# A two-layer graph network on one core: a fourth ring buffer, low halves written over the turned block, and six groups of x projected during the first chunks

## What is computed

```
A = adj + I;  deg = sum(A, axis=1);  d = rsqrt(deg)
A_hat = A * d[:, None] * d[None, :]
x1 = layernorm(x + elu((A_hat @ x) @ w))
x2 = layernorm(x1 + relu((adj @ x1) @ W.T + b))
return x2
```

## Time and profile before

| | |
|---|---|
| median of 3 runs | 890.79 us (888.59 to 893.01) |
| the profiled execution | 887.64 us, span 885.5 us |
| TensorE busy (PE) | 793.9 us, 90% |
| VectorE busy (DVE) | 745.8 us, 84% |
| ScalarE busy (ACT) | 501.5 us, 57% |
| GpSimd busy (POOL) | 172.7 us, 20% |
| read from HBM | 176.8 MB, 204 GB/s over the span |

### The profile page before, as it was taken

One profiled execution on the slowest core, in us unless ns is written; L12 is line 12 of the kernel. 1 busy time (PEld: TensorE's weight loads), 2 busy tenths in 40 slices (PEclk: granted clock), 3 DMA queues, 4 the chain that ended last, 5 costly groups with the idle time before them and its releaser, 6 DMA issues. The chain is left out here.

```text
span 885.5 us, 10755 instructions
## 1 busy us (share of the span) xinstructions
PE 793.9 (90%) x3532; PEld 652.4 (74%) x3532; DVE 745.8 (84%) x611; ACT 501.5 (57%) x1084; POOL 172.7 (20%) x181
## 2 busy tenths in 40 slices
PE   0446959799999999899999999999999989999996
PEld 0335848578878888688887788888888878888885
DVE  2368969899999998788998999898879789888863
ACT  2254546465676673377876745766744565455352
POOL 0003341213442400022210201110210312022021
PEclk9968969899999999899999999999999999999999
DMA  9998987389999649489879778888896887997911
GB/s 272 306 304 215 255 197 172 113 214 274 228 256 281 173 128 273 131 206 227 215 186 253 199 214 202 185 222 194 195 250 172 198 216 186 220 223 171 223 29 30
DMA packets 183590, 181.72 MB, mean 205 GB/s; under 512 B 6768, under 2 KB 183536, under 8 KB 183536
## 3 DMA queue, kind: packets, MB, share of 16 engines
q1 hardware_dynamic: 94704, 93.21, 41.7%
q10 hardware_dynamic: 88832, 87.83, 40.1%
HBM read 176.82 MB, written 4.19 MB: 204 GB/s over the span
## 5 line engine op out<-in xcount | busy, mean ns | idle before, releaser
L967 PE MATMUL acc<-a_hi,v_hi 128*128 128x512 f32 x1024 | 408.6, 399 | 43.4 <-DVE a_lo L638 28.9
L452 ACT ACTIVATE a_hi<-turned 128x1024 fp32r<-128x1024 f32 x256 | 263.9, 1058 | 281.5 <-PE acc L969 126.9
L969 PE MATMUL acc<-a_hi,v_lo 128*128 128x512 f32 x1024 | 402.9, 393 | 0.0
L968 PE MATMUL acc<-a_lo,v_hi 128*128 128x512 f32 x1024 | 402.8, 393 | 0.0
L638 DVE TENSOR_TENSOR a_lo<-turned,a_hi 128x1024 fp32r<-128x1024 f32 x256 | 307.9, 1240 | 32.3 <-ACT a_hi L452 24.2
L621 DVE STREAM_TRANSPOSE turned<-raw 128x2048 f32<-128x2048 f32 x120 | 275.4, 2302 | 26.8 <-DMA raw<-in_adj_dram 21.3
L967 PEld LDWEIGHTS acc<-a_hi,v_hi 128*128 128x128 f32 x1024 | 195.2, 191 | 88.5 <-issue 32.8
L969 PEld LDWEIGHTS acc<-a_hi,v_lo 128*128 128x128 f32 x1024 | 194.7, 190 | 41.4
L968 PEld LDWEIGHTS acc<-a_lo,v_hi 128*128 128x128 f32 x1024 | 195.2, 191 | 39.8
L462 ACT ACTIVATE acc<-raw 128x256 f32<-128x256 f32 x170 | 62.7, 369 | 24.5 <-DMA raw<-in_adj_dram 21.4
L645 DVE TENSOR_REDUCE deg_parts<-raw 128x6 f32<-128x1536 f32 (+3 forms) x28 | 53.5, 1911 | 18.1 <-DMA raw<-in_adj_dram 18.1
(11 more groups left out here) (70 smaller groups left out, 416.1 us busy)
## 6 DMA issues: line engine op xcount, KB each, us to landing
raw<-in_adj_dram SPq DMA_DIRECT2D x152, 512.0 KB, 8.8
raw<-in_adj_dram ACTq DMA_DIRECT2D x152, 512.0 KB, 9.8
x_row<-in_x_dram SPq DMA_DIRECT2D x64, 128.0 KB, 7.1
out_dram<-normed ACTq DMA_DIRECT2D x28, 128.0 KB, 3.3
held<-in_adj_dram ACTq DMA_DIRECT2D x4, 512.0 KB, 12.8
held<-in_adj_dram SPq DMA_DIRECT2D x4, 512.0 KB, 12.8
partial<-in_adj_dram ACTq DMA_DIRECT2D x4, 512.0 KB, 11.9
partial<-in_adj_dram SPq DMA_DIRECT2D x4, 512.0 KB, 14.2
```

The costliest lines, as they stand in the source:

```text
L452: nc.scalar.activation(a_hi[u % 2][:, part, :], turned[u % 2][:, part, :], ACT.Copy).then_inc(s_hi, 1)
L967: pe.matmul(dst, v_hi[:, k, ch], a_hi[u % 2][:, t, :], start=begin, stop=False)
L968: pe.matmul(dst, v_hi[:, k, ch], a_lo[u % 2][:, t, :], start=False, stop=False)
L969: ins = pe.matmul(dst, v_lo[:, k, ch], a_hi[u % 2][:, t, :], start=False, stop=end)
```

## The change

1. A fourth ring buffer `raw3` (home 6). The ring is (0, 1, 6, 2) up to chunk 32 and (0, 1, 6) behind it; chunk (2, 1) has no place of its own any more.
2. `turned` has three buffers and `a_lo` lies at the same addresses: lo(u) overwrites the turned block in place. turn(u) now waits for the product of u-3; lo(u) waits only for hi(u). `a_hi` keeps two buffers.
3. New shares of the row sums: VectorE 10, 10, 6, 3, 3, 4, 4, 4 blocks, GpSimd 5 from group 2 on, ScalarE 6, 6, 5, 8, 8, 7, 7, 7. GpSimd's steps work inside `normed`.
4. x @ w of group g is made at the chunk `X_USED[g]` = 2, 3, 4, 5, 6, 7, 28, 31 for g = 0 to 7: turn_x(g) ends chunk X_USED[g]-1 on TensorE, keep_xt(g) begins ScalarE's part of chunk X_USED[g], project_x(g) begins TensorE's, and a new copy keep_y(g) ends ScalarE's. It frees `proj`: the result is kept in SBUF, in `y_soon` (inside v_lo, groups 0 to 3) or one of two `y_late` (groups 4 to 7). x is loaded straight to these places, two chunks ahead, all on SP's queue; w, W and b are loaded behind chunk 0.
5. The scratch of dynamic DMAs shrinks from 4096 to 256.

```diff
@@ -52,6 +52,7 @@
     RB = GN // B32
     EPS = 1e-5
     JUNK = 2
+    TURNS = 3
...
-    HOMES = {chunk_of[0, 1]: 3, chunk_of[1, 1]: 4, chunk_of[0, 0]: 5, chunk_of[2, 1]: 5}
+    HOMES = {chunk_of[0, 1]: 3, chunk_of[1, 1]: 4, chunk_of[0, 0]: 5}
+    RING = (0, 1, 6, 2)
     buffer_of, before, filled = [], [], []
     for n in range(len(chunks)):
         if n in HOMES:
             home = HOMES[n]
         else:
-            held = [max([k for k in range(n) if buffer_of[k] == i], default=-1) for i in range(3)]
-            free = [(done_at[k] if k >= 0 else -1, i) for i, k in enumerate(held)]
-            home = min(free[:3 if n <= FIRST_B else 2])[1]
+            free = []
+            for i in RING if n <= FIRST_B else RING[:3]:
+                k = max([k for k in range(n) if buffer_of[k] == i], default=-1)
+                free.append((done_at[k] if k >= 0 else -1, i))
+            home = min(free)[1]
...
-    DVE_BLOCKS = [10, 10, 8, 6, 5, 6, 6, 5]
-    POOL_BLOCKS, POOL_FROM = 4, 2 * PANELS
+    DVE_BLOCKS = [10, 10, 6, 3, 3, 4, 4, 4]
+    POOL_BLOCKS, POOL_FROM = 5, 2 * PANELS
+    X_USED = [2, 3, 4, 5, 6, 7, 28, 31]
...
-        turned = [sb(f"turned{i}", [P, GT, GN]) for i in range(2)]
+        raw.append(sb("raw3", [P, RB, STRIPE]))
+        turned_at = -(-nc.sbuf_base // B32) * B32
+        turned = [sb(f"turned{i}", [P, GT, GN]) for i in range(TURNS)]
         a_hi = [sb(f"a_hi{i}", [P, GT, GN], F32R) for i in range(2)]
-        a_lo = [sb(f"a_lo{i}", [P, GT, GN], F32R) for i in range(2)]
+        a_lo = [nc.alloc_sbuf_tensor_at(f"a_lo{i}", [P, GT, GN], F32R, offset=turned_at + 4 * GT * GN * i) for i in range(TURNS)]
...
-        halved = sb("halved", [P, POOL_BLOCKS, STRIPE // 2])
-        quartered = sb("quartered", [P, POOL_BLOCKS, STRIPE // 4])
-        folded = sb("folded", [P, 2, POOL_BLOCKS, STRIPE // 8])
+        halved = normed[:].rearrange("p t n -> p (t n)")[:, 0:POOL_BLOCKS * (STRIPE // 2)].rearrange("p (k m) -> p k m", k=POOL_BLOCKS)
+        folded = normed[:].rearrange("p t n -> p (t n)")[:, POOL_BLOCKS * (STRIPE // 2):POOL_BLOCKS * (STRIPE // 2 + STRIPE // 4)]
+        folded = folded.rearrange("p (i k m) -> p i k m", i=2, k=POOL_BLOCKS)
+        w_kept = partial[:, 0, :, 0:C]
+        y_late = [sb(f"y_late{i}", [P, GT, C]) for i in range(2)]
+        y_soon = nc.alloc_sbuf_tensor_at("y_soon", [P, N // P, C], F32, offset=v_at + 4 * (N // P * C))
...
+        def y_of(row):
+
+            return y_soon[:, tiles(row), :] if row < FAST else y_late[row % 2][:]
...
-                if m >= 1 and m <= GROUPS:
-                    sp.wait_ge(s_xw, m)
-                elif m > GROUPS:
+                if m > GROUPS:
                     sp.wait_ge(s_resx, m - GROUPS)
+                elif m == GROUPS:
+                    sp.wait_ge(s_xw, GROUPS)
+                elif m >= FAST + 2:
+                    sp.wait_ge(s_v, m - 1)
+                into, signal = (y_of(m), s_xin[m]) if m < GROUPS else (x_row[:], s_x)
                 for q in range(STRIPES):
-                    sp.dma_start(x_row[B32 * q:B32 * (q + 1), :, :], nodes_part(x, m % GROUPS, q)).then_inc(s_x, 16)
+                    sp.dma_start(into[B32 * q:B32 * (q + 1), :, :], nodes_part(x, m % GROUPS, q)).then_inc(signal, 16)
...
-                if m <= GROUPS:
-                    n = PANELS * m + (1 if m < FAST else 2)
+                if m < GROUPS:
+                    n = X_USED[m] - 2
+                elif m == GROUPS:
+                    n = FIRST_B + 2
...
-                if n == 1:
+                if n == 0:
                     sp.dma_start(w_sb[:], w.rearrange("(h c) n -> c h n", h=CH)).then_inc(s_w, 16)
-                    sp.dma_start(normed[:, 0:CH, :], W.rearrange("(h c) n -> c h n", h=CH)).then_inc(s_w, 16)
+                    sp.dma_start(w_kept, W.rearrange("(h c) n -> c h n", h=CH)).then_inc(s_w, 16)
                     sp.dma_start(b_sb[:], b.rearrange("(a n) -> a n", a=1).to_broadcast([P, C])).then_inc(s_w, 16)
...
                 if i:
-                    pool.wait_ge(s_quartered, i)
-                nc.gpsimd.tensor_tensor(halved[:], mine[:, :, :STRIPE // 2], mine[:, :, STRIPE // 2:], ALU.add).then_inc(s_halved, 1)
+                    pool.wait_ge(s_folded, i)
+                else:
+                    pool.wait_ge(s_const, 1 + STRIPES)
+                nc.gpsimd.tensor_tensor(halved, mine[:, :, :STRIPE // 2], mine[:, :, STRIPE // 2:], ALU.add).then_inc(s_halved, 1)
                 pool.wait_ge(s_halved, i + 1)
-                if i:
-                    pool.wait_ge(s_folded, i)
-                nc.gpsimd.tensor_tensor(quartered[:], halved[:, :, :STRIPE // 4], halved[:, :, STRIPE // 4:], ALU.add).then_inc(s_quartered, 1)
+                quarter = halved[:, :, :STRIPE // 4]
+                nc.gpsimd.tensor_tensor(quarter, quarter, halved[:, :, STRIPE // 4:], ALU.add).then_inc(s_quartered, 1)
                 pool.wait_ge(s_quartered, i + 1)
                 if i >= 2:
                     pool.wait_ge(s_degp, i - 1)
-                nc.gpsimd.tensor_tensor(folded[:, i % 2, :, :], quartered[:, :, :STRIPE // 8], quartered[:, :, STRIPE // 8:],
+                nc.gpsimd.tensor_tensor(folded[:, i % 2, :, :], quarter[:, :, :STRIPE // 8], quarter[:, :, STRIPE // 8:],
                                         ALU.add).then_inc(s_folded, 1)
...
                 for half, part in HALVES:
                     if u >= 2:
                         act.wait_ge(s_used, halves_of(u - 2, half))
-                        act.wait_ge(s_lo, halves_of(u - 2, half))
-                    nc.scalar.activation(a_hi[u % 2][:, part, :], turned[u % 2][:, part, :],
+                    nc.scalar.activation(a_hi[u % 2][:, part, :], turned[u % TURNS][:, part, :],
...
-                act.wait_ge(s_xw, row + 1)
+                act.wait_ge(s_y, row + 1)
                 if row >= FAST:
                     act.wait_ge(s_turn, max(units_through[n] for n in HOMES))
                 for t in range(GT):
-                    ins = nc.scalar.activation(v_hi[:, tiles(row).start + 2 * t, :], proj[:, t, :], ACT.Copy,
+                    ins = nc.scalar.activation(v_hi[:, tiles(row).start + 2 * t, :], y_of(row)[:, t, :], ACT.Copy,
                                                scale=dinv[:, GT * row + t:GT * row + t + 1])
...
                 act.wait_ge(s_xt_mm, row + 1)
+                if row:
+                    act.wait_ge(s_xw, row)
                 nc.scalar.activation(x_row[:].rearrange("p t n -> p (t n)"), proj[:].rearrange("p t n -> p (t n)"),
                                      ACT.Copy).then_inc(s_xt, 1)
+
+            def keep_y(row):
+
+                act.wait_ge(s_xw, row + 1)
+                nc.scalar.activation(y_of(row), proj[:], ACT.Copy).then_inc(s_y, 1)
...
+                if n in X_USED:
+                    keep_xt(X_USED.index(n))
...
-                if at == (2 if row < FAST else 3):
-                    keep_xt(row)
+                if n in X_USED:
+                    keep_y(X_USED.index(n))
...
-                if u >= 2:
-                    dve.wait_ge(s_hi, halves_of(u - 2, 1))
-                    dve.wait_ge(s_lo, halves_of(u - 2, 1))
+                if u >= TURNS:
+                    dve.wait_ge(s_used, halves_of(u - TURNS, 1))
...
-                    if u >= 2:
-                        dve.wait_ge(s_used, halves_of(u - 2, half))
-                    nc.vector.tensor_tensor(a_lo[u % 2][:, part, :], turned[u % 2][:, part, :],
+                    nc.vector.tensor_tensor(a_lo[u % TURNS][:, part, :], turned[u % TURNS][:, part, :],
                                             a_hi[u % 2][:, part, :].bitcast(F32),
                                             ALU.subtract).then_inc(s_lo, 1)
...
-                pe.wait_ge(s_x, 64 * (row + 1))
+                pe.wait_ge(s_xin[row], 64)
                 if row:
-                    pe.wait_ge(s_v, row)
+                    pe.wait_ge(s_y, row)
                 flat = proj[:].rearrange("p t n -> p (t n)")
                 for h in range(CH):
                     for t in range(GT):
-                        ins = pe.transpose(flat[:, GN * h + P * t:GN * h + P * (t + 1)], x_row[:, t, P * h:P * (h + 1)], ident[:])
+                        ins = pe.transpose(flat[:, GN * h + P * t:GN * h + P * (t + 1)], y_of(row)[:, t, P * h:P * (h + 1)], ident[:])
...
             for n in range(FIRST_B):
                 row, at = divmod(n, PANELS)
-                if row < FAST and at == 2:
-                    turn_x(row)
+                if n in X_USED:
+                    project_x(X_USED.index(n))
                 if row < FAST and at == 3:
-                    project_x(row)
                     fold_degrees(row)
                 for u in visits[n]:
                     if row >= FAST and u == last_in_a[row]:
                         fold_degrees(row)
                     product(u)
-                if row >= FAST and at == 2:
-                    turn_x(row)
```

(6 more changed lines are left out.)

16 lines of the change are left out of this document (9 added, 7 removed).

## The result

The changed kernel takes 924.63 us, the median of 4 runs (923.24 to 924.99), against 890.6 us before on the same chip: ratio 1.0373, interval 1.0345 to 1.0402 (the quotient of the two medians is 1.0382). It is slower by 34 us. The forecast was 899 us, the range 884 to 913: the sign was right, the size was not, and the value lies 11.6 us above the range. The profiled execution took 924.99 us (span 923.1), which is the median within 0.4 us; the profiles before and after are 37.4 us apart.

A forecast was written before the change was run, and what follows sets the result against it. TensorE, busy 90% of the span, was taken as the bound, with its idle stretches. The terms 1.8 + 7.4 + 1.7 + 1 - 3 gave +8.9 us on 887.64, so 896.5; carried to the median 899 us, range 884 to 913.

The forecast's parts named there:

- Step 1: First chunks, group 0: chunk 3 arrives at 43 to 46 us, and the first product starts 7 us later, at 58.4.
- Step 2: Group 1: projections of groups 2 to 5 in a row, 7.0 us a round, put fold_degrees(1) at about 93, +21.5 us.
- side remark on the chunks: Ahead of fold_degrees(1): the chunks are no excuse, as the last of them, chunk 7, comes at some 75 us.
- Step 3: Groups 2 and 3: unit 6 +16 us, unit 12 +11; less 9.3 for two projections, sum so far +1.8.
- v follows as before: Group 2, behind the fold near 130.7 us: v takes as long as before, and unit 6 starts near 141.4.
- -2.1 for the shares and -3.9 for the fold that need not wait for a projection: Ahead of the fold of group 2: fewer VectorE blocks win 2.1 us, no wait for a projection wins 3.9.
- -9.3 for the two projections made early: Behind unit 12: the projections of groups 4 and 5 are already made, winning 2 x 4.64 us.
- Step 4: Groups 4 to 7: folds 4 to 6 30.9 and 35.4 us apart; TensorE's waits, handoffs and ScalarE's hold cost +7.4.
- Step 5: Second pass: y_low(7) +1.7 us, extras +1, third buffer -3, a_lo in place 0, GpSimd's fifth block 0.
- A: Chain of step 2: TensorE's clock falls in the gaps, 10 to 15 us more, 909 to 914 us; chance 0.15.
- B: Pass A: smaller VectorE row sums win, fold_degrees(1) before about 80 us, kernel at 870 to 886 us; chance 0.15.
- C: It evens out: chunk 3 at its old time, step 4's idle covered, third buffer gives 4.3 us: 890; chance 0.23.

The follow-up runs named there:

- e9: The changed kernel with the old shares of the row sums (VectorE 10 10 8 6 5 6 6 5, GpSimd 4): 919.71 us, ratio 1.0311.
- e14: The changed kernel with turn_x of the next group ahead of the products of its chunk, not behind them: 915.38 us, ratio 1.0286.
- e15: The changed kernel with x late, GpSimd waiting for v_lo, old shares and turn_x ahead of the products: 898.23 us, ratio 1.0092.
- e3: The kernel before with a_lo written over the turned block, three buffers, turn waiting for the product of u-3: 901.99 us, ratio 1.0119.
- e5: The changed kernel without its fourth ring buffer, chunk (2, 1) back at its own place: 940.18 us, ratio 1.0559.
- e4: The kernel before with the new shares of the row sums alone: 892.75 us, ratio 1.0009.
- e1: The changed kernel with x @ w of groups 1 to 5 at chunks 6, 10, 14, 18, 22: 914.31 us, ratio 1.0255.

## Why the prediction was wrong

**Step 1** was right in kind and 1.8 us short: unit 0 8.8 us later, not 7. project_x(1) ended at about 50, as counted, but chunk 3 came late and was the last thing waited for:

```profile
48.37 2.82 DVE L672 TENSOR_REDUCE deg_parts<-partial 128x10 f32<-128x2560 f32 x1 [6.49 <-DMA partial<-in_adj_dram]
```

It was there at 48.4, where I had 43 to 46.

**Step 2** was right: fold_degrees(1) at 95.2 for 93, by four projections 7.1 us apart for 7.0. Its side remark on the chunks was not. VectorE waited 5.5 to 5.8 us for each of chunks 5, 6 and 7, and the last was there at 85.7 us, not at 75:

```profile
85.66 2.82 DVE L672 TENSOR_REDUCE deg_parts<-raw 128x10 f32<-128x2560 f32 x1 [5.74 <-DMA raw<-in_adj_dram]
94.01 0.26 DVE L691 TENSOR_REDUCE deg_sums<-deg_parts 128x16 f32<-128x64 f32 x1 [5.53 <-ACT acc L483]
```

The fold waited for ScalarE's share, which stands behind keep_xt in the chain, 5.5 us longer than for VectorE's, so the chain and not the chunk set the time. Of the loss of 34 us the chain is a part: with x placed late again the kernel won 10 us, where the sum had 12.2 (21.5 less the 9.3 of the two projections).

**Step 3 failed**, and most of the error is here: unit 12 came at +28.4, not +11. Of the 27.4 us by which the sum was off at unit 41 (38.3 less 10.9), 2.5 are there at the fold of group 1, 14.9 come between it and unit 12, 7.3 from there to the fold of group 6 and 5.2 up to that of group 7; the stretch behind gives 2.5 back. Three terms were mis-sized.

*"v follows as before"*: v_lo took 5.15, 2.40 and 4.37 us for 1.65, for the reason shown above; the change moves y from `proj` to SBUF, and the sum took y_low's new operand at no price, without naming GpSimd beside it. The diagonal block of group 2 took 2.90 us for 0.90.

*-2.1 for the shares and -3.9 for the fold that need not wait for a projection*: the second came about at group 2. From deg_sum to deg_row it took 1.7 us (136.12 to 137.80), before 4.7 (109.71 to 114.44). But the sums themselves came 40.9 us behind the fold of group 1, before 38.5, and not 2.1 sooner; v_lo of group 1 alone put 3.5 us there. Together the fold of group 2 came 42.3 us behind that of group 1, before 42.9, by the forecast 37.7. From there to unit 6 it took 13.8 us in place of 11.3. From unit 6 to unit 12 it took 49.5 us, forecast 42.1. VectorE's timeline of the changed kernel there:

```profile
179.07 0.32 DVE L679 TENSOR_REDUCE deg_parts<-normed 128x5 f32<-128x160 f32 x1 [2.26 <-POOL normed L408]
180.42 0.27 DVE L691 TENSOR_REDUCE deg_sums<-deg_parts 128x16 f32<-128x64 f32 x1 [1.03 <-ACT acc L483]
...
184.10 2.36 DVE L665 TENSOR_TENSOR a_lo<-turned,a_hi 128x1024 fp32r<-128x1024 f32 x2 [1.19 <-ACT a_hi L473]
186.37 0.15 DVE L699 TENSOR_SCALAR deg<-acc 128x4 f32<-128x4 f32 x1
```

And of the kernel before:

```profile
154.93 0.27 DVE L664 TENSOR_REDUCE deg_sums<-deg_parts 128x16 f32<-128x64 f32 x1 [2.11 <-ACT acc L462]
160.88 0.15 DVE L672 TENSOR_SCALAR deg<-acc 128x4 f32<-128x4 f32 x1
```

The smaller share of VectorE waits for the larger ones of GpSimd and ScalarE. And though TensorE folds 1.7 us behind the sums (182.08) where it took 5.4 before, deg_row comes 5.95 us behind them in both kernels, for it stands behind a_lo of unit 11: here VectorE's own order keeps what the fold gains.

*-9.3 for the two projections made early*: from unit 12 to the fold of group 4 it took 42.9 us with no projection in it and 42.3 with one, from fold 4 to 5 34.0 and 33.2. VectorE set that pace, as step 4 itself said of folds 4 to 6, so TensorE's freed 4.64 us were idle time. Step 4 took back 3.6 of the 9.3; the 5.7 that stayed were to be won between unit 12 and fold 6, and that stretch became 1.6 us longer.

**Step 4 failed.** Folds 4, 5 and 6 are 34.0 and 37.9 us apart, not 30.9 and 35.4. VectorE's busy time between folds 4 and 5 went from 31.7 to 30.8 us, not by 2.3 us, and it waited for GpSimd and ScalarE as well. Its a_lo took longer (1274 ns on average, 1240 before; 1256 in the changed kernel with the old shares, e9), so about half of that comes with the new shares, and the other half is open. VectorE's waits in the changed kernel from 200 to 316 us, and those of the kernel before from 172 to 285:

```profile
DVE deg_parts L679 <- POOL normed L408: 3.8, 2, 1.9
DVE deg_sums L691 <- ACT acc L483: 1.8, 2, 1.2
```

```profile
DVE deg_parts L652 <- POOL folded L386: 1.8, 2, 0.9
DVE deg_sums L664 <- ACT acc L462: 0.5, 1, 0.5
```

The hold of ScalarE at keep_xt was named for chunk 31 and priced at 1.6 us, with 2.2 for the two handoffs; it was 8.8 us at chunk 28 and 7.2 at chunk 31. Folds 6 and 7 are 51.8 us apart, where they were 42.8 and the sum had 46.6. Of the 9 us more, TensorE idles 3.7; the rest is busy time, for some 24 matmuls more stand in this stretch (a turn_x and a project_x), which the sum left out. With turn_x placed first (e14) the stretch takes 46.3 us, 5.4 less, and the whole kernel wins 8 to 9 us by it (e14, e15).

**Step 5** was right ahead of unit 41, where 6.23 us of idle time stand (forecast 6.3, before 4.57), and no transpose waits for a chunk. Behind unit 41 the sum had +1 and -3, so -2; measured, -0.7. That it came so near is luck, for both terms were far too small: the in-place halves cost some 10 us alone (e3), not 2.7, and the buffer beside them wins 8.5 behind unit 41 (e5), not 3. My bound of 4.3 us for it, the idle time of the kernel before, could not hold where another part of the change makes new idle time.

Slips in the working itself are small: by step 3's own terms the fold of group 2 is at 129.6 and not 130.7, eight blocks at 0.27 us are 2.2 and not 2.3, 5.8 less 2 is 3.8 and not 3.6, and 890.79 plus 8.9 is 899.7.

**The rivals.** A (the clock falls in the chain) did not happen: the chain ran at full clock, as below. Its reading that the first projection ran at the low clock rests on the duration (6.66 us for 3.61); the window over it has 1.00. B needed fold(1) ahead of 80 us, and it came at 95.2; its ground, that smaller row sums on VectorE win by themselves, fell with e4 (1.0009). Its rule that every us of fold(1) is one won does not hold either: e1 has the fold 26 us sooner and wins 10. C needed chunk 3 at its old time, 39.0, and it came at 48.4.

## What to carry to other kernels

When an operand moves from PSUM to SBUF, price each of its readers anew: here four VectorE instructions with both inputs in SBUF took 2.4 to 5.2 us beside GpSimd's steps, and 1.66 with one of them in PSUM. A copy that is put ahead in an engine's program holds all that stands behind it, DMA issues among it, for as long as its input is late (8.8 us here); place its producer first (0.33 us). A projection made early frees TensorE only where TensorE sets the pace. Test the parts of such a change one by one: here the ring buffer alone was the best kernel (884.6 us), and the in-place halves that came with it gave the gain back (890.6 us).

## What the runs showed of the hardware that was not expected

The contention can cost more than one GpSimd step: four VectorE instructions (1.65 us for the four before) took 5.15 us, 3.5 us more, beside four steps of GpSimd (2.34, 0.94, 0.59 and 1.56 us), and the halving of 128x640 among them took 2.34 us for 1.56. The diagonal block, four 128x128 additions with both inputs in SBUF in either kernel, took 2.90 us in group 2 beside a halving, and 0.90 in the kernel before, where GpSimd had a step of its own beside the first 0.1 us of it.

TensorE's clock stood through a chain with gaps. Windows of the changed kernel over the chain, and over the start of unit 1:

```profile
69.00:95.00 26.00, 17.93 (x90) 14.40 (x88) 8.20 (x4) 16.71 (x55) 0.00 (x0) 1.00 1.11 286
100.80:105.00 4.20, 4.17 (x10) 3.34 (x11) 4.20 (x4) 1.67 (x3) 3.90 (x4) 0.50 0.80 154
```

Over 26 us TensorE was busy 69% of the time, with turn_x, project_x and gaps of 1.1 and 1.2 us, and the granted clock was 1.00 (2.4 GHz) throughout; project_x took 3.72 us, turn_x 1.04 to 1.07. After 5.35 us of idle time the next product began at 0.50 (1.2 GHz). The Trainium skill ("TensorE: Matmul & The Clock Gate", Part 4: PE-mode transpose) has transposes not count as activity in the same way; by that rule each gap here was 3.4 us long (1.21, 1.06 and 1.11), and the prediction expected the clock to go in that case. If turn_x is such a transpose, the trace does not agree.
